# Attention scores in a transformer layer as three products of high and low fp32r parts, with the order of the steps around them changed

## The reference

```python
q, k = rope(hs @ Wq.T), rope(hs @ Wk.T)        # 16 heads of 128, 256 tokens each
s = clip(hs @ Ws1.T @ Ws2.T + bs2, -32, 32)    # 64 slots per head
z = cumlogsumexp(s over tokens); es = exp(s); enz = exp(-z)
A = where(mask, q @ k.T * 128**-0.5, 0)        # causal scores, no softmax over them
ok = enz * (A @ es); qv = softmax(ok)
W2 = where(mask, (qv * enz) @ es.T, 0)
o = W2 @ v
o_g = o * rsqrt(mean(o * o) + 1e-5) * g_norm_weight * (g * sigmoid(g))
attn = o_g @ Wo.T
mlp = (gelu(hs @ Wgate.T) * (hs @ Wup.T)) @ Wdown.T   # 2048 wide, 4-bit weights
out = x + attn + mlp
```

## Time and profile before

| what | value |
|---|---|
| median of three executions | 1091.55 us |
| profiled execution, own time | 1093.5 us |
| its span, first to last instruction | 1091.5 us |
| mean granted clock of TensorE | 0.995 |
| TensorE busy | 1075.9 us, 99% |
| VectorE busy | 893.2 us, 82% |
| ScalarE busy | 657.8 us, 60% |
| GpSimd busy | 418.5 us, 38% |
| DMA | 23.06 MB, mean 21 GB/s |

### The profile page before, as it was taken

How to read it: one execution, slowest core, us unless ns; L and a number is a source line. 1 busy time by engine, 2 the same in 40 slices (tenths; PEclk the granted TensorE clock), 3 DMA queues, 4 the chain that set the end, 5 groups by cost and what they waited for, 6 DMA issues and landing times.

```text
span 1091.5 us, 20558 instructions
## 1 busy us (share of the span) xinstructions
PE 1075.9 (99%) x7176; PEld 928.4 (85%) x7176; DVE 893.2 (82%) x1680; ACT 657.8 (60%) x2111; POOL 418.5 (38%) x308
## 2 busy tenths in 40 slices
PE   8899999999999999999999999999999999999998
PEld 7688888888888888888888888888888888888887
DVE  6888887888888888788878888778888788888776
ACT  5566565656655766555765556655566665656653
POOL 6252253432524335233542326333253432524331
PEclk9899999999999999999999999999999999999999
DMA  5011000010002000020000200002000020000001
GB/s 171 1 38 43 1 1 1 33 48 1 1 1 79 2 2 1 1 80 2 1 1 2 80 2 2 1 1 80 1 1 1 7 74 1 1 2 1 20 21 39
DMA packets 9542, 23.06 MB, mean 21 GB/s; under 512 B 864, under 2 KB 5856, under 8 KB 8544
## 3 DMA queue, kind: packets, MB, share of 16 engines
q1 hardware_dynamic: 9440, 21.76, 5.7%
HBM read 19.66 MB, written 2.10 MB: 20 GB/s over the span
## 4 chain that ended last, share of the span: by engine, by line
PE 94%; DVE 3%; ACT 1%; issue 1%; POOL 1%; POOLq 0%; DVEq 0%; ACTq 0%
PE bank L219 22%; PE bank L221 21%; PE bank L220 21%; PE bank L386 5%; PE bank L317 5%; PE bank L358 3%; PE bank L330 3%; PE bank L319 3%; PE bank L395 2%; PE bank L349 1%; PE bank L379 1%; PE bank L342 1%; PE bank L367 1%; PE bank L333 1%; PE bank L307 1%
## 5 line engine op out<-in xcount | busy, mean ns | idle before, releaser
L1355 POOL TENSOR_TENSOR inter_lo<-ffb,inter_hi 128x512 fp32r<-128x512 f32 x62 | 78.9, 1295 | 485.9 <-ACT inter_hi L751 485.9
L1346 POOL TENSOR_TENSOR qkT<-ra,xs 128x512 f32<-128x512 f32 x128 | 165.0, 1289 | 105.5 <-DVE xs L1040 83.3
L714 ACT ACTIVATE sm<-bank,mx 128x64 f32<-128x64 f32 x256 | 76.3, 326 | 143.9 <-DVE mx L996 143.9
L1037 DVE TENSOR_TENSOR ra<-bank,rope 128x512 f32<-128x512 f32 x128 | 88.0, 687 | 58.7 <-ACT xs L696 56.8
L985 DVE RECIPROCAL enzT<-enzT 128x256 f32<-128x256 f32 x64 | 111.5, 1743 | 0.0
L695 ACT ACTIVATE xs<-bank 64x512 f32<-64x512 f32 x128 | 76.1, 594 | 56.7 <-PE bank L221 40.5
L219 PE MATMUL bank<-xh,wqk_hi 128*128 128x512 f32 x256 | 106.8, 417 | 0.0
L1040 DVE TENSOR_TENSOR xs<-xs,rope 128x512 f32<-128x512 f32 x128 | 106.8, 834 | 0.0
L219 PE MATMUL bank<-xh,wgu_hi 128*128 128x512 f32 x256 | 105.8, 413 | 0.0
L219 PE MATMUL bank<-wvg_hi,xh 128*128 128x512 f32 x256 | 100.9, 394 | 1.0 <-ACT xh L755 1.0
L221 PE MATMUL bank<-xh,wgu_lo 128*128 128x512 f32 x256 | 101.0, 395 | 0.0
(11 more groups left out here) (165 smaller groups left out, 3054.2 us busy)
## 6 DMA issues: line engine op xcount, KB each, us to landing
raw<-in_w_qkvg SPq DMA_DIRECT2D x7, 1024.0 KB, 7.3
scaled<-in_w_scaled SPq DMA_DIRECT2D x8, 640.0 KB, 8.5
packed<-in_w_packed SPq DMA_DIRECT2D x8, 384.0 KB, 3.1
acc<-in_x SPq DMA_DIRECT2D x4, 512.0 KB, 8.3
out<-acc SPq DMA_DIRECT2D x3, 512.0 KB, 3.3
raw<-in_w_qkvg SPq DMA_DIRECT2D x2, 512.0 KB, 6.4
ws_raw<-in_w_slot SPq DMA_DIRECT2D x8, 48.0 KB, 3.0
rope<-in_rope_tab SPq DMA_DIRECT2D x1, 256.0 KB, 7.5
```

Source lines behind the costliest of these rows:

```text
L714: ins = act.activation(sm[:, c], src[:, c], ACT.Exp, bias=mx[:, g:g + 1], accum_out=ssum[:, g:g + 1])
L1037: dve.tensor_tensor(two(ra[i % 2][:, :]), two(pj[i][:, :]), cos, ALU.mult).then_inc(cos_done, 1)
L1346: pool.tensor_tensor(qkT[:, i, :], ra[i % 2][:, :], xs[i % 2][:, :], ALU.add).then_inc(roped, 1)
L1355: pool.tensor_tensor(dst[1][e], ffb[e][:, :], dst[0][e].bitcast(F32), ALU.subtract).then_inc(inter_lo, 1)
```

## The change

The 256-column product of a score block (all queries of a sequence against its first 128 keys) is made from fp32r parts with `three`. The 128-column product (second half of the queries against the second half of the keys) stays fp32. For this there are new buffers q_s and k_s; k_s holds only the first 128 keys of each sequence. A new ScalarE step `score_hi` copies a tile of qkT to the high part, a new VectorE step `score_lo` subtracts it for the low part; both read SBUF only. There are four of each in a stage: 512 columns for q and 256 for k, for each head. Three of the ScalarE steps stand at the end of the stage before, among the swaps and squares, and one behind the first two off-diagonals. Two of the VectorE steps stand at the end of the stage before, behind the weights' diagonals and between the rotary steps, and two at the start of the stage, around `norm_arg`.

`scores` now does both blocks of one head: two 128-column products, a wait for the low parts (qk_lo), and two times three. The scores of head 1 move behind all four MLP tiles; a v/g tile moves ahead of the slot scores; VectorE's third and fourth `score_diagonal` move behind `gate_arg(1)`; ScalarE's `gate_square(1)` moves ahead of the third `off_diagonal`. In the last stage a MLP tile moves ahead of the slot reads, the second `last_norm` moves ahead of the first `last_gate`, and an addition to acc behind the last gate. The buffers xb, osq and osq1 become one, `spare`. The parts of the diff left out declare buffers and semaphores and place the new steps in the start-up in the same way.

```diff
...
@@ -93,6 +92,8 @@
         esJ = sb("esJ", [P, NT, P])
         okz = sb("okz", [P, TOK])
         qkT = sb("qkT", [P, 4, TOK])
+        q_s = [sb(f"q_{s}", [P, 2, TOK], F32R) for s in ("hi", "lo")]
+        k_s = [sb(f"k_{s}", [P, 2, 2, P], F32R) for s in ("hi", "lo")]
         xs = [sb(f"xs{i}", [P, TOK]) for i in range(2)]
         ra = [sb(f"ra{i}", [P, TOK]) for i in range(2)]
         vS = [sb(f"vS{i}", [P, NT, 256]) for i in range(2)]
@@ -103,8 +104,7 @@
         state = sb("state", [P, 2, DV])
         sm = sb("sm", [P, TOK])
         qe = sb("qe", [P, TOK])
-        osq = sb("osq", [P, TOK])
-        osq1 = sb("osq1", [P, TOK])
+        spare = sb("spare", [P, 2 * TOK])
         og = sb("og", [P, NT * 256])
         ogT = [[sb(f"ogT_{s}{h}", [P, TOK], F32R) for h in range(2)] for s in ("hi", "lo")]
         inter = [[sb(f"inter_{s}{e}", [P, TOK], F32R) for e in range(2)] for s in ("hi", "lo")]
...
@@ -181,8 +182,10 @@
         mlp_raw = raw[:, 0:1024].rearrange("p (k n) -> p k n", k=KT)
         od_raw = raw[:, 1024:2048]
 
+        osq, osq1 = spare[:, 0:TOK], spare[:, TOK:2 * TOK]
+        xb = spare[:, :].rearrange("p (n d) -> p n d", n=NT)
         xn = [og[:, :].rearrange("p (n d) -> p n d", n=NT), G[1][:, :].rearrange("p (n d) -> p n d", n=NT),
-              xb[:, :, :], xb[:, :, :]]
+              xb, xb]
         ws1 = osq[:, 0:KT * P].rearrange("p (k n) -> p k n", k=KT)
         xhl = (xh, xl)
 
@@ -307,17 +310,17 @@
                     mm = pe.transpose(dst[:, i * P:(i + 1) * P], src[:, i * P:(i + 1) * P], ident[:, :])
                 mm.then_inc(E_full, 1)
 
-            def scores(st, bp, i, hp):
-
-                h, b = i // 2, i % 2
-                if b == 0:
-                    pe.wait_ge(roped, 4 * st + 2 * h + 2)
-                dst = sc[b]
-                t0 = b * T
-                pe.matmul(dst[:, 0:T], qkT[:, 2 * h + 1, t0:t0 + P], qkT[:, 2 * h, t0:t0 + T],
-                          start=True, stop=True)
-                pe.matmul(dst[:, T:T + P], qkT[:, 2 * h + 1, t0 + P:t0 + T], qkT[:, 2 * h, t0 + P:t0 + T],
-                          start=True, stop=True).then_inc(A_full, 1)
+            def scores(st, h):
+
+                pe.wait_ge(roped, 4 * st + 2 * h + 2)
+                for b in range(2):
+                    wait(pe, *((W_diag, 2 * st - 1 + b) if h == 0 else (A_off, 4 * st + b + 1)))
+                    t = slice(b * T + P, (b + 1) * T)
+                    pe.matmul(sc[b][:, T:T + P], qkT[:, 2 * h + 1, t], qkT[:, 2 * h, t], start=True, stop=True)
+                pe.wait_ge(qk_lo, 4 * st + 2 * h + 2)
+                for b in range(2):
+                    three(pe, sc[b][:, 0:T], [k[:, h, b, :] for k in k_s],
+                          [q[:, h, b * T:(b + 1) * T] for q in q_s], True, True).then_inc(A_full, 1)
 
             def slot_reads(st, bank):
 
@@ -527,32 +530,32 @@
                 if first:
                     mlp_up(st, bp, hp, 0)
                     mlp_up(st, bp, hp, 1)
-                for i in (0, 1):
-                    if first and i == 1:
-                        pe.wait_ge(h1_done, 4)
-                        pe.wait_ge(h1_lo, 2)
-                    if not first:
-                        pe.wait_ge(W_diag, 2 * st - 1 + i)
-                    scores(st, bp, i, hp)
+                if first:
+                    pe.wait_ge(h1_done, 4)
+                    pe.wait_ge(h1_lo, 2)
+                scores(st, 0)
                 if first:
                     mlp_up(st, bp, hp, 2)
                 else:
                     mlp_up(st, bp, hp, 0)
                     mlp_up(st, bp, hp, 1)
-                for i in (2, 3):
-                    pe.wait_ge(A_off, 4 * st + i - 1)
-                    scores(st, bp, i, hp)
                 if not first:
                     mlp_up(st, bp, hp, 2)
-                mlp_up(st, bp, hp, 3)
+                    mlp_up(st, bp, hp, 3)
+                scores(st, 1)
+                if first:
+                    mlp_up(st, bp, hp, 3)
                 if first:
                     pe.wait_ge(es_ready, 1)
                     slot_transpose(rg[0], esT[0])
                 if not first:
                     gated_transpose(st)
+                if not first:
+                    project_vg(st + 1, nbp, nhp, 0, True)
                 pe.wait_ge(A_off, 4 * st + 3)
                 slot_scores(st, nbp, nhp)
-                project_vg(st + 1, nbp, nhp, 0, True)
+                if first:
+                    project_vg(st + 1, nbp, nhp, 0, True)
                 project_vg(st + 1, nbp, nhp, 1, True)
                 if not first:
                     pe.wait_ge(ogT_hi, 2 * st - 1)
@@ -596,19 +599,15 @@
             each_stage(pe, stage)
 
             st, bp, hp = LAST, LAST_BP, HP - 1
-            for i in (0, 1):
-                pe.wait_ge(W_diag, 2 * st - 1 + i)
-                scores(st, bp, i, hp)
+            scores(st, 0)
             mlp_up(st, bp, hp, 0)
-            for i in (2, 3):
-                pe.wait_ge(A_off, 4 * st + i - 1)
-                scores(st, bp, i, hp)
             mlp_up(st, bp, hp, 2)
+            scores(st, 1)
+            mlp_up(st, bp, hp, 1)
             slot_reads(st, sc[0])
             slot_states(st, bp)
             gated_transpose(st)
             slot_rows(st)
-            mlp_up(st, bp, hp, 1)
             mlp_up(st, bp, hp, 3)
             pe.wait_ge(inter_lo, 2 * st)
             previous_outputs(0, (2, 3), sc[0])
@@ -695,6 +694,17 @@
                 act.activation(xs[i % 2][0:64, :], pj[i][64:128, :], ACT.Copy)
                 act.activation(xs[i % 2][64:128, :], pj[i][0:64, :], ACT.Copy).then_inc(swapped, 1)
 
+            def score_hi(n, i):
+
+                act.wait_ge(roped, 4 * n + i + 1)
+                h = i // 2
+                if i % 2 == 0:
+                    ins = act.activation(q_s[0][:, h, :], qkT[:, i, :], ACT.Copy)
+                else:
+                    ins = act.activation(k_s[0][:, h, :, :],
+                                         qkT[:, i, :].rearrange("p (b t) -> p b t", b=2)[:, :, 0:P], ACT.Copy)
+                ins.then_inc(qk_hi, 1)
+
             def slot_exp(n, par):
                 act.wait_ge(clip_done, n + 1)
                 act.activation(esT[par][:, :], esT[par][:, :], ACT.Exp).then_inc(es_ready, 1)
...
@@ -804,8 +816,10 @@
                 prep = st + 2 if st < 2 else None
                 if first:
                     gate_square(st, 0)
+                    score_hi(0, 2)
                 off_diagonal(st, 0)
                 off_diagonal(st, 1)
+                score_hi(st, 3)
                 if not first:
                     gate_square(st, 0)
                 gate_tanh(st, 0)
@@ -819,11 +833,14 @@
                     prepare_scales(hp + 1)
                 if bp == 3 and more:
                     split_hi(hp + 1, W_VG)
+                if not first:
+                    gate_square(st, 1)
                 off_diagonal(st, 2)
                 if bp == 3 and more:
                     split_hi(hp + 1, W_QK)
                 off_diagonal(st, 3)
-                gate_square(st, 1)
+                if first:
+                    gate_square(st, 1)
                 if first:
                     x_scale_act(prep)
                 if not first:
@@ -861,9 +878,12 @@
                 if bp == 2 and more:
                     split_slot(hp + 1)
                 copy_J(st + 1, rg[1][:, :])
+                score_hi(st + 1, 0)
                 swap_halves(st + 1, 2)
+                score_hi(st + 1, 1)
                 swap_halves(st + 1, 3)
                 square_o(st, 0)
+                score_hi(st + 1, 2)
                 square_o(st, 1)
 
             each_stage(act, stage)
@@ -925,6 +946,17 @@
                 mask = mask_w[:, 0, :].unsqueeze(1).to_broadcast([P, NT, P])
                 dve.tensor_tensor(Wt[h][:, :, :], src, mask, ALU.mult).then_inc(W_diag, 1)
 
+            def score_lo(n, i):
+
+                dve.wait_ge(qk_hi, 4 * n + i + 1)
+                h = i // 2
+                if i % 2 == 0:
+                    ins = dve.tensor_tensor(q_s[1][:, h, :], qkT[:, i, :], q_s[0][:, h, :].bitcast(F32), ALU.subtract)
+                else:
+                    ins = dve.tensor_tensor(k_s[1][:, h, :, :], two(qkT[:, i, :])[:, :, 0:P],
+                                            k_s[0][:, h, :, :].bitcast(F32), ALU.subtract)
+                ins.then_inc(qk_lo, 1)
+
             def norm_arg(done):
 
                 dve.wait_ge(ms_done, 2 * done)
...
@@ -1147,26 +1181,32 @@
                 prep = st + 2 if st < 2 else None
                 score_diagonal(st, 0)
                 score_diagonal(st, 1)
+                score_lo(st, 2)
                 if first:
                     clip(0, 0, rg[0][:, :])
                     x_bias(prep)
                 else:
                     norm_arg(st)
+                score_lo(st, 3)
                 gate_arg(st, 0)
                 if first:
                     gate_gelu(st, 0)
```

(22 more changed lines are left out.)

## The result

The changed kernel took 1121.53 us (median of four, 1120.85 to 1122.51) against 1091.53 us of the kernel before on the same chip; the ratio is 1.0273, with a 95% interval of 1.0261 to 1.0285. It is slower by 30 us. The forecast was 1121.4. The profiled execution took 1121.5 us with a span of 1119.6, against 1093.5 and 1091.5: +28.0 and +28.1. The 2 us between the two ways of counting are the profiled execution of the kernel before, which took 2 us more than its median; they are taken up at the end.

What follows compares the result with a forecast made beforehand. TensorE was taken to bound every steady stage. Stages 1 to 30 sum to 15 x 0.66 + 8 x 1.17 + 7 x 1.5 = 29.8 us, first and last nothing; 1091.55 + 29.8 = 1121.4 us, range 1105 to 1137.

Steps and rivals of the forecast that it cites:

- 1. third sine product ends: Stage change, VectorE: score_lo(0) is held until the second rotation ends at −1.96; third tile's sine ends about −0.16, before −1.0.
- 2. score_lo(1) done: score_lo(1) takes 0.34, to 0.18, in time for TensorE at 0.44; third rotation waits for it, ends 1.47, before 0.41.
- 3. fourth sine product ends: VectorE's fourth sine product needs the shared port, ends at 2.0, before 0.96; fourth rotation 2.15 to 3.45.
- 4. score_lo(2) done: score_lo(2), ready at 2.7, is held by the fourth rotation to 3.45, ends 4.0; squares end 3.2, not deciding.
- 5. mse starts: Norm on VectorE: mse at 4.2 instead of 2.44, then the 1.65 us GpSimd power, scal at 6.1 instead of 4.37.
- 6. hidden(0) starts: After scal: hidden(0) at 9.0, gate_arg(1) at 9.6, score_diagonal(2) 10.2 to 10.6, ScalarE's off_diagonal(2) done at 11.0.
- The saving on TensorE: Score blocks: three fp32r products cost 0.354 instead of 0.44 us, saving 0.34 a stage, 11.0 us in 32 stages.
- The held instructions: VectorE instructions with two SBUF operands and GpSimd's exclude each other; the one issued second waits for all of the first.
- Index 3: Stages of round index 3: a 1.05 us ScalarE weight split delays gated_hi(0), gated_lo(0) and slot reads to 13.6; net +1.5.
- A: Rival: TensorE stays covered because VectorE has 6.6 us free a stage; full −11.0, 1080.5 us; chance 0.18.
- B: Rival: subtractions and rotations do not hold each other; index 0 and 2 −0.3, 1 +0.2, 3 +0.6; 1093 us; chance 0.14.
- C: Rival: GpSimd takes the port first at score_lo(1), scores wait 1.2 us; +1.5 a stage, 1138 us; chance 0.08.

Runs made afterwards that it cites:

- the first experiment: Kernel before, with the 256-column score products as three fp32r products of constant-filled tiles, nothing added on ScalarE or VectorE: 1084.17 us, ratio 0.9932.
- fourth experiment: Changed kernel with the subtractions reading their first operand from PSUM instead of SBUF (low parts wrong), MLP tiles waiting for them: 1095.65 us, ratio 1.0031.
- third: Changed kernel without the four VectorE subtractions a stage, low parts constant, ScalarE's copies and all moves kept: 1086.15 us, ratio 0.9954.
- the last experiment: Changed kernel with norm_arg and diagonals earlier, dequantisation behind scal, q/k split earlier, next v/g split before gate_tanh(0), its GpSimd half behind scal: 1089.39 us, ratio 0.9976.

## Why the prediction was right

The forecast was 1121.4, the measurement 1121.53. By the prediction's own steps, in stage 16 (expected, measured from 580.48):

| step | expected | measured |
|---|---|---|
| 1. third sine product ends | −0.16 | −0.22 |
| 2. score_lo(1) done | 0.18 | 0.11 |
| 2. third rotation ends | 1.47 | 1.25 |
| 3. fourth sine product ends | 2.0 | 1.81 |
| 3. fourth rotation ends | 3.45 | 3.24 |
| 4. score_lo(2) done | 4.0 | 3.79 |
| 5. mse starts | 4.2 | 3.90 |
| 5. scal starts | 6.1 | 5.94 |
| 6. hidden(0) starts | 9.0 | 8.92 |
| 6. diagonal(2) starts | 10.2 | 10.13 |
| slot reads start | 12.75 (12.09 + 0.66) | 12.72 |

**The saving on TensorE** (0.34 us a stage) was right, shown by the first experiment alone, undisturbed by the rest.

**The held instructions** were right, and shown from both sides: with one operand in PSUM the same subtractions run beside the rotations (fourth experiment), and without them stages of index 0 and 2 are covered (32.52) and the others within 0.2 and 0.3 us of it (third). The third rotation was taken to wait for score_lo(1) until 0.18 and then to last its whole length, as the rule for VectorE turned round. It began at −0.10 beside it and lasted 1.35 instead of 1.27: it lost 0.08 us, not 0.23. This one error of 0.2 runs on through the table; at mse it is 0.3, since msn began before score_lo(2) had ended.

**The power held by score_lo(3)** was in the prediction as an uncertainty of up to 0.2: it is 0.10 (1.75 against 1.65), and it cancels part of the other error.

**The sum.** From the starts of all stages, stages 1 to 30 are 27.9 us longer than before, where 29.8 was forecast. Index 1: eight stages, +9.4 (9.4 forecast). Index 0 and 2: fifteen stages, +9.6 (9.9). Index 3: seven stages, +8.9 (10.5); this term was mis-sized, 1.27 a stage for 1.5. Slot reads began at 559.67 − 546.35 = 13.32 there, not at 13.6:

```profile
557.14 1.05 ACT L662 ACTIVATE wqk_hi<-raw 128x1024 fp32r<-128x1024 f32 x1
558.09 0.27 ACT L729 ACTIVATE At<-bank 128x128 f32<-128x128 f32 x1
558.25 1.09 ACT L747 ACTIVATE ogT_hi<-bank 128x512 fp32r<-128x512 f32 x2
...
558.88 0.69 DVE L989 TENSOR_TENSOR ogT_lo<-bank,ogT_hi 128x512 fp32r<-128x512 f32 x1 [1.61 <-ACT ogT_hi L747]
...
559.67 0.65 PE L333 MATMUL bank<-At,esJ 128*64 128x256 f32 x4 [0.49 <-ACT ogT_hi L747]
```

I had added the lengths of ScalarE and VectorE instructions that follow each other, and each starts about 0.1 before the last one ends. What they waited for is right: gated_hi(0) and then gated_lo(0) behind the weight split. The view of waits names ogT_hi (seven waits of 0.5 us), but the half that the slot reads need was written before 558.88; the ogT_lo of 558.88 ends at 559.57, 0.1 before they start, and is what they waited for last. The first stage came out at −0.1 and the last at +0.3, both taken at nothing. So the misses do not cancel in the stages: by the profiled executions the error is 1.8 us (1123.3 forecast, 1121.5 measured), and that the medians differ by 0.1 only is chance: the profiled execution of before lay 2 us above its median, that of after on it.

**The rivals.** A (all covered) did not come about, but its floor of 32.51 is real. B's stages are what the fourth experiment measured. C did not occur: VectorE took the port first. The time that separates the forecast from A was never VectorE's busy share, 119.67 of the 135.17 us of four stages or 89%: it was where on its chain four instructions stood.

## What to carry to other kernels

When one engine is the bound with no idle time, price a change by the chain of waits that will reach it last, not by the busy shares of the helpers: here 1.9 us more a stage on an engine with 6 us to spare made the bounding one wait 1.0 us in the lightest stages and 1.3 in the mean of stages 1 to 30 (1018.6 us against 981.0 in the first experiment). Look for instructions that exclude each other and for what stands behind them in their queues; here an instruction with two SBUF operands beside a long GpSimd instruction cost the rest of that instruction. A PSUM operand removed the hold (0.68 us beside a rotation), where there is a right value in PSUM to read; another place in the queue moved part of it to the next GpSimd instruction (2.01 for 1.75 us). After a move on one chain, the next of several waits that lie close together takes over (og, gate_gelu, A_off here), so one move alone gives only part of the gain (11 and 18 us here, 26 together), and the last few us come only when each of the waits is gone.

## What was not expected of the hardware

GpSimd behind VectorE lost less than VectorE behind GpSimd. The third rotation of stage 16 began at 580.38 and the subtraction ahead of it ended at 580.18 + 0.41 = 580.59: an overlap of 0.21 us, for 0.08 more than the 1.27 of before. Over all stages the third rotation has a median of 1.27 us before and 1.35 after. The power began at 584.63 and the subtraction beside it ended at 584.88: 0.25 us, for 0.10 more than 1.65. The Trainium skill (SBUF — State Buffer, "Who interferes with whom") says that the one issued second waits for the whole of the first. For a VectorE instruction behind a rotation the traces agree: it ended 0.55 us behind the rotation both times, for a length of 0.68 of its own. For the power and the third rotation the loss was 0.08 of 0.21 and 0.10 of 0.25 us of overlap, so they did not wait for the whole of the subtraction as the profile shows it. Whether the GpSimd instruction has a part that goes on without the port, or the subtraction gives it up before its record ends, no run here tells.

The granted clock of TensorE in the start-up is not the same from one kernel to the next, nor between executions of one kernel. Two microseconds of the kernel before, then of the changed one, columns as above:

```profile
54.00:56.00 2.00, 1.36 (x6) 0.73 (x5) 2.00 (x2) 2.00 (x13) 0.00 (x0) 0.50 0.00 0
```

```profile
54.00:56.00 2.00, 1.33 (x6) 0.75 (x4) 1.40 (x2) 2.00 (x12) 0.00 (x0) 1.00 0.03 8
```

A clock of 0.50 is 1.2 GHz, 1.00 is 2.4. In the kernel before it fell soon after 52: TensorE was busy for 0.85 us from 50 to 52, at a clock of 1.00, and for all 2.00 us from 52 to 54, at 0.57. In the changed kernel it was busy for 0.59 and 0.85 us of the same two stretches, and the clock stayed at 1.00. What decides it the runs do not show. Of fifteen executions of the kernel before in the first group, thirteen had a mean clock of 0.997 or 0.998 and took 1090.9 to 1092.3 us; two had 0.995 and took 1093.4 and 1093.6. That is 2 us more, as much as the last experiment gains by medians. The mean clock is not all of it: in the other two groups one execution of the kernel before took 1091.6 at 0.995, and one 1092.8 at 0.998. Small differences between kernels of this kind are safer read from steady stages: from stage 8 on, those of one index repeat within 0.1 us in the kernel before and in the changed one.
